# Attention sums transposed in two groups of eight over two PSUM banks, in a hybrid transformer kernel on one Trainium2 core

## What is computed

```
x = x + encoder(layernorm(x))        # 4 layers of: attention with ALiBi and causal mask, feed-forward; final layernorm
x = x + experts(layernorm(x))        # 8 experts, the 2 nearest of each row
x = x + rope_attention(layernorm(x)) # causal, rotary positions, 16 heads of 8
x = x + experts(layernorm(x))

# every attention, per head h (16 heads of 8 features):
attn = softmax(q @ k.T / sqrt(8) + mask)
out  = attn @ v                      # then all heads side by side, times Wo
```

## Time and profile before

| | us |
|---|---|
| median of 3 runs | 2695.03 |
| lowest and highest run | 2693.42, 2697.32 |
| the profiled execution | 2701.02 |
| its span | 2699.2 |
| TensorE busy in the span | 2307.5 (85%) |
| VectorE busy | 1758.7 (65%) |
| ScalarE busy | 1466.4 (54%) |
| GpSimd busy | 901.2 (33%) |

### The profile page before, as it was taken

How to read it: one execution, slowest core, us unless ns; L and a number is a source line. 1 busy time by engine, 2 the same in 40 slices (tenths; PEclk the granted TensorE clock), 3 DMA queues, 4 the chain that set the end, 5 groups by cost and what they waited for, 6 DMA issues and landing times.

```text
span 2699.2 us, 106822 instructions
## 1 busy us (share of the span) xinstructions
PE 2307.5 (85%) x46638; PEld 1434.7 (53%) x46638; DVE 1758.7 (65%) x5525; ACT 1466.4 (54%) x2646; POOL 901.2 (33%) x1037
## 2 busy tenths in 40 slices
PE   3789999999999999999988887968878788879983
PEld 1345555555555555555555544866644444447873
DVE  6878787777777778777888753323657677643112
ACT  0367777777777777777655554432244334454431
POOL 6233343334333433333333332223122332221135
PEclk9699999999999999999999888988989788889986
DMA  4253333333433333423122203566421221205764
GB/s 114 80 162 114 101 120 108 119 111 102 129 103 115 116 117 106 127 92 114 57 73 76 68 19 101 165 177 183 132 64 59 65 64 59 63 12 178 212 194 112
DMA packets 162546, 289.02 MB, mean 107 GB/s; under 512 B 28504, under 2 KB 116312, under 8 KB 160344
## 3 DMA queue, kind: packets, MB, share of 16 engines
q1 hardware_dynamic: 153696, 264.23, 32.2%
q0 software_dynamic: 8384, 17.97, 2.4%
HBM read 227.33 MB, written 95.96 MB: 120 GB/s over the span
## 4 chain that ended last, share of the span: by engine, by line
PE 62%; DVE 18%; ACT 7%; issue 5%; POOL 2%; DMA 2%; another core or an unknown queue 2%; SPq 2%; POOLq 0%; ACTq 0%; DVEq 0%
PE bank L461 24%; PE bank L612 10%; PE bank L566 9%; DVE mx L1240 6%; PE bank L754 5%; PE bank L764 5%; PE bank L636 3%; ACT big L845 3%; PE bank L468 2%; DVE stats L927 1%; PE bank L574 1%; ACT OT L851 1%; DVE xn L940 1%; PE bank L642 1%
## 5 line engine op out<-in xcount | busy, mean ns | idle before, releaser
L845 ACT ACTIVATE big<-bank 128x512 f32<-128x512 f32 x1600 | 923.4, 599 | 748.5 <-PE bank L461 671.9
L1240 DVE TENSOR_REDUCE mx<-bank 128x16 f32<-128x512 f32 (+1 forms) x1440 | 897.9, 655 | 416.3 <-PE bank L574 368.2
L461 PE MATMUL bank<-QS,KS 99*32 99x512 bf16 (+3 forms) x10240 | 648.4, 310 | 46.0 <-ACT big L845 34.1
L566 PE MATMUL bank<-KS,QS 96*32 96x352 bf16 (+15 forms) x10240 | 587.7, 292 | 105.9 <-DVE mx L1240 66.0
L1538 POOL TENSOR_SCALAR_AFFINE_SELECT big<-big 128x768 f32<-128x768 f32 (+1 forms) x416 | 254.2, 634 | 647.8 <-ACT big L845 647.8
L612 PE MATMUL bank<-big,V 128*9 128x512 f32 (+3 forms) x5120 | 446.3, 444 | 16.5 <-ACT big L845 10.8
L566 PEld LDWEIGHTS bank<-KS,QS 96*32 96x32 bf16 x10240 | 240.3, 98 | 409.0 <-DVE mx L1240 180.7
L461 PEld LDWEIGHTS bank<-QS,KS 99*32 99x32 bf16 x10240 | 216.7, 99 | 214.5 <-ACT big L845 86.4
L574 PE MATMUL bank<-mask_a,ident_b 128*32 128x64 bf16 (+1 forms) x5760 | 305.8, 195 | 12.3 <-issue 12.2
L913 ACT ACTIVATE big<-bank,big 128x256 f32<-128x256 f32 x368 | 151.0, 470 | 266.0 <-PE bank L754 209.6
L754 PE MATMUL bank<-big 128*128 128x256 f32 x736 | 186.3, 398 | 34.8 <-ACT big L898 18.2
(11 more groups left out here) (216 smaller groups left out, 2895.8 us busy)
## 6 DMA issues: line engine op xcount, KB each, us to landing
big<-e_pack SPq DMA_DIRECT2D x92, 578.0 KB
QS<-part_scr SPq DMA_DIRECT2D x480, 96.0 KB
KS<-part_scr SPq DMA_DIRECT2D x480, 96.0 KB
part_scr<-parts SPq DMA_DIRECT2D x80, 384.0 KB
x_rows<-in_alibi SPq DMA_DIRECT2D x47, 384.0 KB, 5.2
y_rows<-in_alibi SPq DMA_DIRECT2D x47, 384.0 KB, 5.8
big<-x_rows SPq DMA_DIRECT2D x92, 128.0 KB
y_rows<-big SPq DMA_DIRECT2D x92, 128.0 KB
```

The lines of the kernel that those rows point to most:

```text
L461: last = mm(out[c:c + 32], stationary[:, c:c + 32], moving, start=start, stop=stop)
L566: mm(bk[h * SUB:(h + 1) * SUB, col:col + w], Q[0:ROW_MAX, 4 * quad + h, i * SUB:(i + 1) * SUB], K[0:ROW_MAX, 4 * quad + h, 0:w], start=(co ...
L845: A(dst, src, ACT.Exp).then_inc(exp_done, 1)
L1240: v.tensor_reduce(mx[:, quad, k, 0:w], src, axis=AX.X, op=ALU.max).then_inc(a_used, 1)
```

## The change

The four groups become two pairs: t0 and t1 at position 7, t2 and t3 at position 11. Even groups go to bankR, odd groups to bankPV, the bank of the value products. The reciprocals get two halves of rl, so that n1 doesn't overwrite what n0 reads. `normalise` moves to positions 8, 9, 12 and 13. t1 no longer waits for anything of its own, t2 waits for n0 and t3 for n1. As bankPV now holds transposed sums, pv0 waits for all four `normalise` of the job before, where it waited for the last `evac_ot` of that job.

```diff
-        rl = sb("rl", [P, H])
+        rl = sb("rl", [P, 2, H])
+        bankN = [bankR, bankPV]
...
-                        if j > 0 or g > 0:
+                        if g > 0:
                             pe.wait_ge(ot_done, QUADS * (b + j) + g)
+                        elif j > 0:
+                            pe.wait_ge(norm_done, TT * (b + j))
...
-                    else:
-                        pe.wait_ge(norm_done, TT * (b + j) + t)
+                    elif t >= 2:
+                        pe.wait_ge(norm_done, TT * (b + j) + t - 1)
                     for g in range(QUADS):
-                        last = nc.tensor.transpose(bankR[:, g * P:(g + 1) * P], OT[:, g, t * P:(t + 1) * P], ident[:])
+                        last = nc.tensor.transpose(bankN[t % 2][:, g * P:(g + 1) * P], OT[:, g, t * P:(t + 1) * P], ident[:])
...
-                extras += [(lambda b, j, t=t: ot_transposes(b, j, t), -1, (7 + 2 * t, 1)) for t in range(TT)]
+                extras += [(lambda b, j, t=t: ot_transposes(b, j, t), -1, ((7, 7, 11, 11)[t], 1)) for t in range(TT)]
...
-                    heads = bankR[:].rearrange("p (h c) -> p h c", h=H)
+                    heads = bankN[t % 2][:].rearrange("p (h c) -> p h c", h=H)
-                    ch.link(v.reciprocal(rl[:], heads[:, :, HD]))
+                    ch.link(v.reciprocal(rl[:, t % 2, :], heads[:, :, HD]))
...
-                extras += [(lambda b, j, t=t: normalise(b, j, t), -1, (8 + 2 * t, 0)) for t in range(TT)]
+                extras += [(lambda b, j, t=t: normalise(b, j, t), -1, ((8, 9, 12, 13)[t], 0)) for t in range(TT)]
```

More of the change, by code:

```diff
@@ L1281, in normalise @@
                     v.tensor_tensor(attn[:, t, :].rearrange("p (h d) -> p h d", h=H), heads[:, :, 0:HD],
-                                    rl[:].unsqueeze(2).broadcast_to([P, H, HD]), ALU.mult).then_inc(norm_done, 1)
+                                    rl[:, t % 2, :].unsqueeze(2).broadcast_to([P, H, HD]), ALU.mult).then_inc(norm_done, 1)
                 def add_x(b, j):
```

## The result

| | kernel before | changed |
|---|---|---|
| median of 7 runs each, us | 2693.6 | 2705.7 |
| lowest and highest | 2686.5, 2697.3 | 2700.3, 2715.9 |
| span of the profiled execution | 2699.2 | 2707.9 |
| TensorE busy in it | 2307.5 | 2303.2 |
| one plain encoder job, t0 to t0 | 45.73 | 46.30 |

The ratio is 1.0049, with a 95% interval of 1.0032 to 1.0066: the changed kernel is slower by some 12 us.

The account below looks back on a forecast made before the run. It took the plain jobs' TensorE, and whichever wait ends last there (pv0 for n3 through VectorE's queue), as the bound: 11.0 - 1.2 - 2.8 = +7.0 us on 2695.0 gives 2702 us, range 2690 to 2712.

Parts of the forecast that it names:

- Part 1: Plain jobs, TensorE from b8 to a10 and b13 to a14: its own work gets shorter by 0.65 us a job.
- Part 2: Plain jobs, ScalarE behind the first pair: b10 waits 0.39 us and, like a11, comes 0.09 us later.
- Part 3: Plain jobs, pv0 waits 0.7 us for n3; each job 0.44 us longer, +11.0 us over 25.
- the chain: VectorE's queue from the maximum of a11 through n2, the cast of split2 and n3 to pv0: 3.25 us.
- the collision with GpSimd: Plain jobs, cast of split2 slowed beside GpSimd's subtraction: between 0 and 0.59 us a job, taken as 0.
- Nothing is given back later: Rest of a plain job behind pv0: no later wait absorbs the delay, so all 0.44 us stand.
- Part 4: Jobs that route, from 1300 us on: pv0 some 2.3 us earlier in three, little of it kept; -1.2 us in all.
- The other half of the argument: Route jobs: TensorE stands over 2 us before pv0, so the half-clock stretch falls on pv0 and chunks behind it.
- Part 5: Rotary jobs: pv0 earlier by 0.55 us in five jobs, -2.8 us in all (between -3.5 and 0).
- faster: Rival: n3 is done before TensorE reaches pv0, keeping nearly all 0.65 us a job; 2675 us, chance 0.18.
- no net change: Rival: b10 doesn't wait, so pv0 is only 0.09 us a job later; 2693 us, chance 0.27.
- Slower still: Rival: the split2 cast collides with GpSimd in every plain job; up to 2717 us, chance 0.10.

Follow-up runs that it names:

- e1: Changed kernel with the banks in another order (t0 and t3 in bankR, t1 and t2 in bankPV), pv0 needing n2 only; ratio to the kernel before 0.9934.
- e7: e1 with the first pair at position 9 instead of 7, n0 and n1 at position 10; plain job 45.25 us, ratio to the kernel before 0.9924.
- e3: Changed kernel with its first pair undone, t1 back at position 9 and n1 at 10; plain job 46.13 us, ratio to the kernel before 1.0021.
- e2: Kernel before with only the new wait of pv0 for all four normalise added; plain job 46.79 us, ratio to the kernel before 1.0118.
- e9: Kernel before with GpSimd's scatters to the experts replaced by memsets, those rows left out of the result; 2616.3 us, ratio 0.970.
- e10: e1 with GpSimd's scatters to the experts replaced by memsets; jobs 26 to 28 were 1.8, 1.5 and 2.5 us shorter than in e9.
- e4: Kernel before with the second bank alone, positions unchanged, t0 and t2 in bankPV, t1 and t3 in bankR; ratio to the kernel before 0.9962.

## Why the prediction was right

The forecast was 2702 us, and slower; measured were 2705.7, slower, and by the wait that it named. As a change it was too small, +7.0 us against 12.1 between the medians; part of that difference is hidden in the total, since the forecast counted from 2695.0 and the kernel before had a median of 2693.6 in all seven runs. Point by point:

- **Part 1, TensorE's own gain of 0.65 us.** The rows of the changed kernel give it directly. From b8 to a10 are 622.38 - 621.95 = 0.43 us (1.18 before), and the pair takes 1.03 up to a8 where t0 took 0.58. From b13 to a14 are 0.22 us (1.01 before), and the second pair takes 1.02 up to a12 where t2 took 0.59. That is 0.75 - 0.45 = 0.30 and 0.79 - 0.43 = 0.36 us. But the forecast missed a wait that eats 0.15 of it: with t3 moved away, b14 comes too soon for the exponential of b12. It starts 0.18 us behind the last part of a14, L575 (627.10 against 626.92), where it took 0.03 before (621.64 against 621.61). In the timeline of PEld its weight load has the idle time:

```profile
627.10 0.12 PEld L462 LDWEIGHTS bank<-QS,KS 99*32 99x32 bf16 x8 [0.23 <-ACT big L848]
```

So without the wait for n3 TensorE is at pv0 6.56 us behind t0 (e1), not at the forecast's 621.60 - 615.21 = 6.39. With b14's wait the sums close: 0.65 - 0.15 = 0.50 us for both pairs, and 0.48 measured in e7.
- **Part 2, ScalarE.** b10 was reckoned at 2.26 us behind t0 and stood at 2.27. Its price, 0.39, measured 0.38 between e1 and e7.
- **Part 3, pv0.** It was reckoned at 7.09 us behind t0 and stood at 7.23. Two terms of the chain were too small. From the product of n3 to pv0 I took the 0.34 us between such a product and a group of transposes; before the value products it is 0.43 (627.57 to 628.00). And from the cast of `split2` to what follows it took 0.37 us, not 0.33: the collision with GpSimd that I had put at nothing is there, with 0.04 us of the possible 0.59 (0.45 us long at 626.92, 0.42 before, and 0.42 again in e3, where the cast of `split1` stands ahead of n1 as before). Together 0.13 us a job, 3.3 us in 25. That the wait itself came out so close, 0.67 us against 0.70, is in part luck: pv0 was 0.14 us too early in the forecast, and TensorE without the wait 0.17 us too early.
- **Nothing is given back later** in a plain job: shown by e2, where a wait of 1.05 us lengthened the job by 1.06.
- **Part 4, the route jobs.** -1.2 us forecast, -6.6 and -1.8 in two profiles. The 0.3 us for each of jobs 26 and 27 (0.35 and 0.26, 0.29 and 0.24 measured) came out right by luck, for pv0 isn't 2.3 us earlier in jobs 26 to 28: it is 0.64 to 0.72 earlier (10.2 us behind t0, 10.9 before). The term that failed is again the cast of `split2`, priced at nothing. In job 27 of the changed kernel, first DVE, then two rows of POOL, then PE:

```profile
1441.12 1.95 DVE L1204 CAST parts<-resid 128x512 bf16<-128x512 f32 x1
1440.54 1.03 POOL L1498 DMA_INDIRECT x_rows<-xnR,slots  x1 [0.20 <-issue]
1441.61 1.16 POOL L1531 TENSOR_TENSOR parts<-resid,parts 128x512 bf16<-128x512 f32 x1
1443.71 1.90 PE L615 MATMUL bank<-big,V 128*9 128x512 f32 x8 [2.95 <-DVE attn L1284]
```

The cast ends 0.30 us behind GpSimd's subtraction and takes 1.95 us where it took 0.42, so 1.53 of the 2.3 us are gone before pv0, and 0.59 is not the most that such a collision costs. The other half of the argument holds: TensorE stands 2.95 us before pv0, and the value products behind it take 1.90 us, 1.05 in a plain job.
- **Job 25,** which I gave 0.2 us, is 1.8 and 1.7 us shorter. pv0 is 0.19 us earlier in it; the rest goes with the granted clock. Windows over the whole job, from t0 to t0: the kernel before, e9 (the same kernel in this job, as no scatter runs in it yet), then e1 and e10, a pair of the same kind. After the busy times of the engines comes the mean granted clock:

```profile
1301.67:1359.65 57.98, 53.75 (x1259) 32.51 (x1255) 48.71 (x179) 34.95 (x59) 14.62 (x13) 0.94 0.22 66
1299.75:1356.13 56.38, 52.13 (x1258) 31.63 (x1254) 48.64 (x179) 34.97 (x59) 14.64 (x13) 0.97 0.23 67
1298.95:1354.07 55.12, 51.76 (x1258) 31.94 (x1254) 48.64 (x179) 34.97 (x59) 14.63 (x13) 0.97 0.24 68
1297.87:1354.59 56.72, 53.36 (x1259) 32.99 (x1255) 48.76 (x179) 34.94 (x59) 14.63 (x13) 0.94 0.23 67
```

In both pairs pv0 stands at the same place, and the job is 1.60 us longer where the mean clock is 0.94 and not 0.97. Both profiles of the changed kernel have 0.97, the one of the kernel before 0.94, while e9 has 0.97. So the 1.6 us go with a longer or shorter stretch at 1.2 GHz; that the change shortens it isn't shown.
- **Part 5, the rotary jobs.** pv0 earlier by 0.55 us was forecast; it is 0.60 us earlier in all five (9.57 in place of 10.17 us). The 2.8 us that were to come of it aren't seen: the five jobs together are 2.3 us shorter in the first profile and 0.7 us longer in the second. The steps of single jobs vary by more than that, so neither is the gain refuted.

Of the rivals, *faster* fell by part 3, and *no net change* by part 2. *Slower still* was the right mechanism with a fifteenth of its price in the plain jobs, and more than its price in three of the route jobs. With e4 a second bank alone made the kernel 0.38% faster. The rule of the Trainium skill that the prediction weighed (PSUM — Partial Sum Buffer, "Summary: rules for kernel authors"), to read from another bank than the one being written, agrees with that in its own place.

## What to carry to other kernels

A second buffer that is borrowed brings its owner's next user into the wait. Before taking it, follow the queue on the engine that has to empty it, and let the last group to be emptied be in a bank that nobody needs soon: here turning round two banks in a list of four, with the two waits that go with it, took the ratio to the kernel before from 1.0049 to 0.9934. And a gain from grouping work of one kind counts only if the work pushed back isn't what another engine with two buffers is waiting for: the same pair two positions later cost no such wait (e7).

## What the hardware showed unexpectedly

- GpSimd's indirect DMAs that scatter rows, 1.0 us each on an engine that is busy for a third of the time, cost the whole kernel 2695.3 - 2616.3 = 79.0 us when counted by leaving them out (e9 and the kernel before on the same chip, ratio 0.970 with an interval of 0.966 to 0.974). Leaving them out takes their transfers away too, so what of this is GpSimd's queue isn't separated. Jobs 26 and 27 fell from 61.7 to 57.4 and 58.7 us, and others by up to 16. While GpSimd issues scatters and gathers back to back, VectorE and TensorE have idle times that the trace puts down to nothing ("issue"), in the job of this row up to 1.5 us on TensorE and 4.1 on VectorE. The cause isn't shown. The row is from a rotary job of the kernel before:

```profile
2111.60 0.69 DVE L1240 TENSOR_REDUCE mx<-bank 128x16 f32<-128x512 f32 x1 [4.14 <-issue]
```

- The same cast on VectorE took 0.42 us alone, 0.45 beside the end of GpSimd's work, 1.01 in a rotary job and 1.95 us behind a scatter and a subtraction. Where GpSimd's subtraction ran beside it, it ended 0.29 to 0.30 us behind that.
- From the start of a product on VectorE to the start of the work on TensorE that waits for it, it was 0.34 us ahead of transposes and 0.43 us ahead of the value products. Why these differ isn't shown.
